# Channel attention in straight code, with the weights rounded and split at another place in the unit

## The reference

```python
for i in range(len(IDX_LIST)):                     # two halves of 256 columns, each with its own weights
    s, e = (bounds[i], bounds[i + 1])
    h = jnp.einsum('od,bdl->bol', Wq_list[i], z1ss[:, :, s:e])
    h = h + jnp.einsum('od,bdl->bol', Wi_list[i], u1ss[:, :, s:e])
    chunks.append(h)
q, k, v = jnp.split(jnp.concatenate(chunks, axis=2), 3, axis=1)
...
score = jnp.einsum('bndi,bndj->bnij', q + r_w_bias[None, :, :, None], k) * SCALE
prob = jax.nn.softmax(score, axis=-1)
attn_vec = jnp.einsum('bnij,bndj->bndi', prob, v)
attn_out = jnp.einsum('od,bdl->bol', Wo, attn_vec.reshape(bsz, N_HEAD * D_HEAD, qlen)) + bo[None, :, None]
x = attn_out + z1ss
return (x - m) * jax.lax.rsqrt(var + LN_EPS)       # mean and variance over the 256 rows
```

## Time and profile before

| | |
|---|---|
| median of 3 runs | 3975.63 µs (3975.25 to 3976.13) |
| the profiled execution | 3976.29 µs, of it 3974.5 in the span from first to last instruction |
| granted TensorE clock, mean | 0.951 |
| TensorE busy | 3498.8 µs (88%) |
| VectorE, ScalarE, GpSimd busy | 2360.8 (59%), 1817.0 (46%), 2002.5 µs (50%) |
| DMA | 190.08 MB, mean 48 GB/s |
| channel attention | some 208 to 1690 µs of the span; its 64 units lie between 257 and 1640 |

### The profile page before, as it was taken

One profiled execution on the slowest core, in us unless ns is written; L12 is line 12 of the kernel. 1 busy time (PEld: TensorE's weight loads), 2 busy tenths in 40 slices (PEclk: granted clock), 3 DMA queues, 4 the chain that ended last, 5 costly groups with the idle time before them and its releaser, 6 DMA issues. The chain is left out here.

```text
span 3974.5 us, 63693 instructions
## 1 busy us (share of the span) xinstructions
PE 3498.8 (88%) x23616; PEld 2692.5 (68%) x23616; DVE 2360.8 (59%) x2915; ACT 1817.0 (46%) x4207; POOL 2002.5 (50%) x1018
## 2 busy tenths in 40 slices
PE   8979999999999999679999995899957888888876
PEld 5868677767867877368777774788845555555543
DVE  2445555555565555467778775555438677766771
ACT  1135554554455555357667674444422332333321
POOL 1135554564556556436556653555425555555562
PEclk9989999999999999889999997999979989998988
DMA  4231211111121111120021113000030000000000
GB/s 137 64 141 54 71 48 56 65 66 56 43 76 54 55 43 54 43 78 28 33 70 62 39 36 107 16 21 21 21 132 14 1 17 17 17 18 1 12 11 16
DMA packets 108158, 190.08 MB, mean 48 GB/s; under 512 B 13408, under 2 KB 32096, under 8 KB 106720
## 3 DMA queue, kind: packets, MB, share of 16 engines
q1 hardware_dynamic: 105696, 181.97, 13.4%
q10 hardware_dynamic: 2176, 4.19, 0.3%
HBM read 160.97 MB, written 25.17 MB: 47 GB/s over the span
## 5 line engine op out<-in xcount | busy, mean ns | idle before, releaser
L825 POOL TENSOR_TENSOR l_pr<-l_pr,l_inv 128x1024 f32<-128x1024 f32 x256 | 486.0, 1919 | 411.5 <-DVE l_inv L885 411.5
L734 ACT ACTIVATE l_pr<-l_ps_s,l_top 128x512 f32<-128x512 f32 x512 | 347.6, 693 | 354.3 <-DVE l_top L881 300.9
L1255 POOL TENSOR_TENSOR tok_pr<-tok_pr,tok_ma 128x1024 f32<-128x1024 f32 x128 | 305.0, 2405 | 284.1 <-DVE tok_pr L1620 283.9
L2374 POOL TENSOR_TENSOR rec_rs<-rec_sE,rec_rT 128x1024 f32<-128x1024 f32 x128 | 321.8, 2515 | 248.7 <-DVE rec_sE L2761 246.5
L820 POOL TENSOR_TENSOR l_x_lo<-l_zu,l_x_hi 128x2048 fp32r<-128x2048 f32 x63 | 288.3, 4576 | 233.5 <-ACT l_x_hi L718 233.5
L881 DVE TENSOR_REDUCE l_top<-l_ps_s 128x2 f32<-128x1024 f32 x256 | 301.2, 1217 | 19.1 <-PE l_ps_s L582 16.8
L592 PE MATMUL l_ps_t<-l_ident,l_pr 128*128 128x128 f32 x2048 | 280.1, 280 | 25.4 <-ACT l_pT L739 14.6
L2761 DVE TENSOR_TENSOR_SCAN rec_sE<-rec_wE,rec_ps_v 128x1024 f32<-128x1024 f32 x128 | 292.7, 2286 | 4.9
L592 PEld LDWEIGHTS l_ps_t<-l_ident,l_pr 128*128 128x128 f32 x2048 | 225.0, 142 | 103.3 <-issue 77.0
L1501 ACT ACTIVATE tok_pr<-tok_pr,tok_shift 128x256 f32<-128x256 f32 x512 | 253.6, 498 | 13.5 <-DVE tok_shift L1628 12.6
L739 ACT ACTIVATE l_pT<-l_ps_t 128x512 f32<-128x512 f32 x256 | 153.9, 601 | 78.0 <-PE l_ps_t L592 78.0
(11 more groups left out here) (374 smaller groups left out, 10178.7 us busy)
## 6 DMA issues: line engine op xcount, KB each, us to landing
l_zu<-x SPq DMA_DIRECT2D x64, 512.0 KB, 3.7
l_zu<-in_c SPq DMA_DIRECT2D x64, 512.0 KB, 4.6
l_w_raw<-in_L_w_qk SPq DMA_DIRECT2D x16, 512.0 KB, 7.2
tok_xs<-x SPq DMA_DIRECT2D x16, 512.0 KB, 4.0
x<-tok_xb SPq DMA_DIRECT2D x16, 512.0 KB, 2.8
l_xt<-in_xT SPq DMA_DIRECT2D x8, 512.0 KB, 6.5
l_ct<-in_cT SPq DMA_DIRECT2D x8, 512.0 KB, 8.1
l_xn<-in_x SPq DMA_DIRECT2D x8, 512.0 KB, 4.6
```

What stands on the lines that cost most here:

```text
L734: act.activation(pr[t][:, h, :], ps_s[:, t % 2, h, :], ACT.Exp, bias=top[:, t, h:h + 1], accum_out=mass[:, t, h:h + 1]).then_inc(exped, 1)
L825: pool.tensor_tensor(pr[t][:, :, :], pr[t][:, :, :], inv[:, t, :].unsqueeze(2).to_broadcast([P, 2, FEAT]), ALU.mult).then_inc(scaled, 1)
L1255: pool.tensor_tensor(tile, tile, ma[u][:, :, :].rearrange("p t k -> p (t k)").unsqueeze(1).to_broadcast([P, 2, TT * TOK]), ALU.add).then_i ...
L2374: pool.tensor_tensor(rs[j % 2][:, :, :], sE[j % 2][:, :, :], rT[s][:, :, :], ALU.mult).then_inc(rs_made, 1)
```

## The change

`each_pass` no longer makes a hardware loop: it is a Python loop, so that the 48 units of passes 1 to 3 stand in the program one after the other like those of pass 4. In those passes `g` becomes a number, so the waits compare with constants, and `add` asks for `g == COUPLES` in place of "is it a number". On ScalarE, `round_wv` moves from ahead of `keep_turned(g, b, 2)` to behind `keep_turned(g, b, 3)`, `round_w(0)` to the same place (both ahead of `round_keys`), and `round_w(1)` to behind `round_keys`. On VectorE, `split_wv` and `split_w(0)` move to behind `keep_turned(g, b, 3)`, and `split_w(1)` to behind `split_keys`. Nothing is added or removed: the instructions that compute are the same, in the same unit.

```diff
@@ each_pass
-            with eng.Fori(1, COUPLES) as g:
+            for g in range(1, COUPLES):
                 for i in range(UNITS):
                     unit(g, i, lambda d: True)
@@ ScalarE's unit
                 if there(1):
                     exponentials(g, b + 1, 0)
-                if b == BATCH and there(UNITS):
-                    round_wv(g + 1)
                 keep_turned(g, b, 2)
                 if there(1):
                     exponentials(g, b + 1, 1)
                 if there(2):
                     round_queries(g, b + 2)
                 keep_turned(g, b, 3)
+                if b == BATCH and there(UNITS):
+                    round_wv(g + 1)
+                if b % BATCH == 5 and there(BATCH):
+                    round_w(0, weights_at(g, b) + 2)
                 if there(2):
                     round_keys(g, b + 2)
+                if b % BATCH == 5 and there(BATCH):
+                    round_w(1, weights_at(g, b) + 2)
                 if b % BATCH == 0:
                     round_wo(g, b)
                 if there(3):
                     round_inputs(g, b + 3)
                 round_output(g, b)
-                if b % BATCH == 5 and there(BATCH):
-                    round_w(0, weights_at(g, b) + 2)
...
                     exponentials(g, b + 1, 3)
-                if b % BATCH == 5 and there(BATCH):
-                    round_w(1, weights_at(g, b) + 2)
@@ VectorE's add
-                    if isinstance(g, int) and b >= BATCH:
+                    if g == COUPLES and b >= BATCH:
@@ VectorE's unit
                     tops(g, b + 1, 1)
-                if b == BATCH and there(UNITS):
-                    split_wv(g + 1)
                 keep_turned(g, b, 2)
...
                 keep_turned(g, b, 3)
+                if b == BATCH and there(UNITS):
+                    split_wv(g + 1)
+                if b % BATCH == 5 and there(BATCH):
+                    split_w(0, weights_at(g, b) + 2)
                 if b % BATCH == 0:
                     split_wo(g, b)
                 if there(2):
                     split_keys(g, b + 2)
+                if b % BATCH == 5 and there(BATCH):
+                    split_w(1, weights_at(g, b) + 2)
                 split_output(g, b)
...
                     inverse(g, b + 1, 2)
-                if b % BATCH == 5 and there(BATCH):
-                    split_w(0, weights_at(g, b) + 2)
...
                 add(g, b)
-                if b % BATCH == 5 and there(BATCH):
-                    split_w(1, weights_at(g, b) + 2)
```

## The result

The changed kernel takes 3932.8 µs in the median (3925.65 to 3938.82, 4 runs), before 3975.88 (3975.25 to 3985.19, 4 runs): a ratio of 0.9891, 95% interval 0.9869 to 0.9912. It is faster by 1.1%, and the time lies 4.7 µs under the forecast of 3937.5, within its range.

What follows compares the result with a forecast made beforehand. TensorE was taken as the bound in channel attention, busy 1328.64 of 1383 µs. Gains of 13.8 + 12.5 + 11.9 = 38.2 µs from 3976.29 gave 3938.1, or 3937.5 for the median; range 3929 to 3951.

Steps and rivals of the forecast that it cites:

- Unit 8: Passes 1 to 3: moving the value weights' rounding and split removes two waits ahead of `turn`; gain 13.8 µs.
- Units 13 and 14: Passes 1 to 3: moving query and key weights' work removes 3.07 µs of TensorE waits, laid to the key split; gain 12.5.
- The pass borders: Unit 15 to unit 0 into passes 2 and 3: without the loop both cost 23.58 µs; gain 11.9.
- The moved work costs nothing at its new place: Roundings and splits at new places in units 5, 8 and 13: costed at nothing, with 0.2 µs spare ahead of `round_output`.
- the steady units of the loop and of pass 4 agree to 0.05 µs, so I count nothing for register arithmetic: Steady units of the passes: removing the loop's register instructions was counted as no gain.
- The sum: All 64 channel attention units: 13.8 + 12.5 + 11.9 = 38.2 µs gained.
- The part behind: The 2334 µs after channel attention, unedited: its clock may win or lose 8 µs when it starts 38 µs earlier.
- a sign of being wrong: Part behind 1600 µs: the prediction is wrong if it differs from its 2334 µs by more than 8.
- straight code starving TensorE: Rival, passes 2 and 3: late instruction fetches at eight places, 6.4 µs each, give 3989 µs; 4%.
- the wait only changes its name: Rival, units 8 and 14: the turn waits for copies of other work, parts 1 and 2 give nothing, 3964 µs; 5%.
- the edge stays: Rival, pass borders: the 3.90 µs come with a pass's first units, not the branch; 3949.5 µs; 4%.
- the moved work costs at its new place: Rival, units 5, 8 and 13: moved roundings lose time, 3950.5 µs, or 3966 with every split slow; 8%.

Runs made afterwards that it cites:

- e1: Kernel before with the weights' roundings and splits at their new places, hardware loop kept on all engines: 3948.85 µs, ratio 0.9924.
- e7: Changed kernel with rounding and split of the key weights (part 1) back at the unit's end on both engines: 3939.6 µs.
- e12: Changed kernel with query weights' rounding and split back late in the unit, each part having its own semaphore: 3932.17 µs.
- e3: Changed kernel with TensorE alone keeping the hardware loop, the other four engines straight: 3941.06 µs, ratio 0.9900.
- e4: Changed kernel with TensorE alone in straight code, the other four engines keeping the loop: 3946.39 µs, ratio 0.9915.
- e5: Changed kernel with VectorE alone keeping the hardware loop: 3944.06 µs.
- e11: The changed kernel run once more, unaltered, for the part behind channel attention: 3930.9 µs, ratio 0.9893.
- e2: Kernel before with straight code on all engines, roundings and splits at their old places: 3954.38 µs, ratio 0.9934.
- e9: Changed kernel with query weights' rounding and split back late in the unit, both roundings sharing one semaphore count: 3949.99 µs.
- e6: Changed kernel with ScalarE alone keeping the hardware loop: 3928.41 µs.

## Why the prediction held

- **Unit 8** was forecast at 13.8 µs and gave 13.9: 70.14 before, 56.27 after, for three; some 0.3 of it is the effect of straight code below (e1, with the loop, gives 13.6). The rounding fills ScalarE's idle time and runs over a little, as forecast:

```profile
445.13 1.96 ACT L707 ACTIVATE l_wv_hi<-l_w_raw 128x2048 fp32r<-128x2048 f32 x1
447.06 0.60 ACT L728 ACTIVATE l_k_hi<-l_ps_b 128x512 fp32r<-128x512 f32 x1
```

- **Units 13 and 14** were forecast at 12.5 and gave 13.1 (136.16 less 123.07), of it 0.3 by the effect below (e1: 12.75). The size is right, the mechanism only in part. The prediction derived the whole 3.07 µs of waiting from the key split at the unit's end. That split makes only the wait of 2.24, 2.3 µs in e7; the 0.83 is the query split's, which slows GpSimd's scaling (0.8 in e12). As the change moved both, the sum did not show it: that is luck. The 1.62 µs between passes 1 and 3 are the clock's, as forecast: 0.91 over 560 to 580 µs, and 1.00 over 1266 to 1290.
- **The pass borders** were forecast at 11.9 and gave 11.9. The forecast's reading of "issue" as TensorE's own late instructions is right: its loop alone costs 4.5 and 6.0 µs (e3). It missed that VectorE stalls beside it and would have kept 1.2 to 1.6 µs of each border by itself (e4, e5); since all engines' loops went together, the sum did not depend on it.
- **The moved work costs nothing at its new place**, as costed. The tightest margin was forecast at 0.2 µs ahead of `round_output` in unit 5; ScalarE's row there, after, beside 1.22 in the earlier trace rows:

```profile
389.58 0.60 ACT L744 ACTIVATE l_o_hi<-l_ps_a 128x512 fp32r<-128x512 f32 x1 [0.28 <-PE l_ps_a L606]
```

The splits meet GpSimd hardly any more: the worst of 16 takes 1362 ns, and took 2911.

```profile
L867 DVE TENSOR_TENSOR l_w_lo<-l_w_raw,l_w_hi x16: 1224/1226/1362, 220.8 to 1402.9; 128x1024 fp32r<-128x1024 f32 x16
```

- **The step that was off** is "the steady units of the loop and of pass 4 agree to 0.05 µs, so I count nothing for register arithmetic". Straight code saves 0.1 µs in each unit without values: 1.6 µs in units 7 and 9 to 12 of three passes. The 0.15 of unit 6, three times, comes in e1 as well and so is not the loop's. The earlier trace rows hid the saving: pass 4 has the longer `add` of line 917 (0.74 µs against 0.68) from unit 8 on, and its units 9 to 12 take 18.84. I compared units that differed in two things with opposite signs. Unit 7 of pass 4, straight and with the short `add`, takes 18.75 in the kernel before, where it takes 18.88 in the loop; that pair would have told. That the `add` makes all of the 0.09 is argued, no run changed it alone.
- **The sum**: 38.2 forecast for the units, 42.4 in the first trace and 40.8 in the second (1359.0 less 1318.2). The parts are 13.9 + 13.1 + 11.9 = 38.9, and 2.0 in units 6, 7 and 9 to 12. The rest, up to 1.4 µs, is in pass 4's last units, which no edit touched and which differ as much between two traces of one kernel.
- **The part behind** was put at plus or minus 8 µs. The kernel before has 2335.0 behind its units. Five of the other 13 traces lie more than 8 below that, the lowest 10.6, so the bound was a little narrow; it sets the spread of every total here. The first trace of the changed kernel is one of the five: its row from 1599 µs on is 2324 long and not 2334, ten less, which the prediction had named as a sign of being wrong. In e11's trace the difference is 6.5. That the total came within 4.7 µs of the forecast is partly luck: the units gave some 3 to 4 µs more than forecast, and the part behind could only be bounded. Of the rivals, straight code starving TensorE is refuted by e2 and the changed kernel: no gap, no longer unit, save unit 8 in e2 by its clock. That the wait only changes its name is refuted by e1, that the edge stays by e2, and that the moved work costs at its new place by units 5, 8 and 13 of the changed kernel.

## What to carry to other kernels

A hardware loop with a long body can be priced from its own trace: subtract the step across the exit from the one across the back edge, and look at each engine's "issue" gap there, not only at that of the busiest one. Work that is needed late (the next weights) belongs behind the copy that frees a bank, in the hole where its engine waits for a long product anyway; a trace with a pass that lacks this work shows both the hole's width and the time that will be left. When units are compared to price one effect, compare those that differ in nothing else, and read a few per mille from unit times in the trace rather than from totals, whose spread here is 17 µs. And where two halves of a change add up to the whole, look whether the parts do.

## What the runs showed of the hardware

- VectorE's subtraction of two SBUF tiles and GpSimd's scaling don't share: who starts second stands nearly still until the first has ended. A split that starts 0.16 µs ahead of the scaling keeps its 1.20 µs, and the pair of scalings takes 4.65 in place of 3.75 (e12). A split that starts inside a scaling takes 2.42 (e7) or 2.91 µs (kernel before), or 3.86 beside `split_inputs` (e9). In each of these three it ends 1.07 to 1.08 µs behind GpSimd's instruction, however long the two overlap (1.35, 1.83 and 2.78 µs), and GpSimd's takes no longer for it (3.75 in e7, 4.56 in e9). The 1.37 µs of some other splits follow the same way from an overlap of 0.28.
- VectorE in straight code has its `add` 0.35 µs late in unit 4 of pass 1 and unit 2 of pass 3, at the same two places in each kernel where its queue is straight (changed, e2, e3, e6 to e12), and never where it is looped (before, e1, e4, e5). Unit ends there are 23.9 and then 23.2 apart, so TensorE loses nothing. In the changed kernel (a unit earlier and a unit later the same `add` has no such idle time ahead of it):

```profile
376.47 0.69 DVE L920 TENSOR_TENSOR l_acc<-l_ps_a,l_acc 128x512 f32<-128x512 f32 x1 [0.45 <-PE l_ps_a L623]
```

The profile names TensorE, but the last product into `ps_a` had ended at 376.00, so the delay is VectorE's own. This fits a late fetch in the middle of straight code, small and hidden, where VectorE's idle time at a back edge is 2.3 to 2.7 µs; no run here tells it from another cause. The Trainium skill ("Runtime: NRT & Kernel Launch", section "Instruction fetch mechanics") says that what it costs to cross a block boundary in straight code is mostly hidden.
- The same two waits of 1.6 to 1.7 µs cost 3.8 µs in one unit and 5.2 to 6.1 in another, by whether the granted clock falls to 1.2 GHz behind them (rows above, 0.83 over 20 µs; 0.56 over 7 µs in the earlier trace rows).
